# Two images in flight on one core: another order of the stages and another merge of the two streams, and routing's token sum made with the norm's transposes

## The chip, the cores and the metric

The kernel runs on one core of a Trainium2 chip. A core has a matrix engine (TensorE, PE in the profile; its weight loads are PEld), a vector engine (VectorE, DVE), a scalar engine (ScalarE, ACT), GpSimd (POOL) and SyncE (SP), which here issues all transfers. Each engine runs its own instructions in order and waits on semaphores for the others. The metric is the time of one execution on the device, in microseconds; the median of a few runs counts.

## The reference, cut to what matters

64 images of 3 x 224 x 224 go through a small vision transformer of two layers, width 192, all in float32:

```python
h = tokens(x, W, b) with class token, + pos_embed            # (64, 197, 192)
h = h + attn0(layernorm(h))      # one head: softmax(q k / sqrt(192)) v
h = h + moe(layernorm(h))        # top 1 of 3 experts for each IMAGE, gelu, width 768
h = h + attn1(layernorm(h))      # 12 heads of 16, projection with bias
h = h + ffn1(layernorm(h))       # patches: gelu MLP of width 768; 6 first tokens: routed atoms

# in moe: the image's mean over its tokens chooses the expert
scores = softmax(mean(x, axis=1) @ Wg.T);  sel = top_1(scores)
out    = (gelu(x @ W1[sel] + b1[sel]) @ W2[sel] + b2[sel]) * scores[sel]
```

The mean over tokens is what the change calls the token sum: the kernel sums the 197 tokens and divides by 197 afterwards.

## The kernel before, in words

An image's 197 tokens lie as two tiles of 99 rows (one of padding). Two images are in flight, one for each of two streams, "a" (p = 0) and "b" (p = 1); each stream has its own buffers and its own four PSUM banks. 32 pairs of images go through. What is done for an image is a list of 57 named stages, STAGES. The names that matter here:

- x: the pixels of both images are transposed by PE in six parts, DVE and ACT copy them to xT in turn (L991, L1207). tok0, tok1: the token matmuls; DVE adds the position (L994).
- statN, normN, turnN: layer norm N. stat is DVE's bn_stats and bn_aggr (L967, L972), then a power on POOL (L600, L602); norm is four tensor_scalar on DVE (L981); turn is PE's transposes (L680), a copy of the high part by ACT (L1216) and the low part by DVE (L1007). Norms 1 and 4 are turned into tokT, norms 2 and 3 into xnT.
- q0, v0, s0, p0, o0: attention 0. q0's result is copied by ACT (L1210) and its remainder made by DVE (L1013).
- route: the expert's choice. DVE sums xnT's transposes over the tokens (xsum, L1037), PE multiplies by Wg, and seven small DVE instructions with one ACT exponential give the expert and its weight (L1040 to L1054). load: SP loads that expert's weights, 2.1 MB, the first part into the tile `shared`.
- hid0_0 to hid0_2, out0_0, out0_1: the expert. hid1, out1: the MLP of layer 1.
- qk1_0, qk1_1, v1: q, k and v of attention 1. ACT copies a high part (hi, L1240), DVE makes a low part (low, L1066), and SP stacks both by nine transfers into q_stack and the k part of `shared` (L516 to L522).
- max0 to max5, maxT: row maxima of the scores of two heads each (PE L809, DVE L1075); maxT turns them and SP places them (L525, L526).
- att0 to att13: scores of head s (PE L827) and its exponential on ACT (L1251); att5, att9 and att13 also multiply the values of four heads (PE L840) and DVE normalizes them: shuffle, reciprocal, multiply (L1084, L1086, L1088). This is called a head group below.
- proj: projection (PE), added to the residual by DVE (L1091).
- regroup: seven copies on POOL that prepare the next pair's pixels.

The streams are half a pair apart: stream b begins at stage B_FIRST = 30. A string MERGE says, letter by letter, whether the next stage is taken from a's list, from b's or from the regroups. The merged list ORDER is one for all engines: each runs its part of every stage in that order, in a loop over the pairs. No engine can take a later stage first, and PE's next stage starts when its semaphores allow, so the order alone decides what stands between a producer and its consumer. A stage's name in AHEAD means that it belongs to the next image of the stream.

In the order before, the middle of a period reads, with b's stages primed and the regroups left out:

```
... att12' turn2' att13' qk1_0 qk1_1 v1 stat1 route' norm1 proj' load' turn1 stat4' q0 v0
norm4' max0 turn4' max1 max2 hid1_0' hid1_1' max3 hid1_2' max4 max5 out1_0' out1_1' ...
```

and the same with the streams changed half a period later. "First half" below is the half with a's qk1_0 and max0, "second half" the one with b's.

What waits for what, on PE: route for xsum, proj for the third head group's normalization, turn1 for norm1, q0 for tokT, max0 for the stacking transfers, for v0's copy and for q0's remainder. load's transfers wait for proj, since they overwrite the k part of `shared`.

## Time and profile before

| | |
|---|---|
| median of 3 runs | 3438.12 us (3432.95 to 3445.44) |
| the profiled execution, its own time | 3436.12 us |
| its span, first to last instruction | 3434.3 us |
| busy share | PE 85%, PEld 77%, DVE 59%, ACT 39%, POOL 10% |
| mean granted clock of PE | 0.932 of full |
| transfers | 287.5 MB, mean 84 GB/s |

Busy time is the time in which an engine's instructions run. Matmuls are pipelined and a waiting matmul can count as busy, so PE's idle time is read from the timeline as well: a number in square brackets there is the idle time of the engine before the instruction, with what ended it. "xN" is a count of instructions merged into the row. PEclk is the share of full clock that PE was granted in the stretch: 1.0 is 2.4 GHz, 0.5 is 1.2 GHz. In a windows row the columns are the stretch, its length, then busy time and instruction count of each engine in the order of the header, PEclk, the mean busy share of the 16 DMA engines and GB/s.

### The profile page before, as it was taken

The page shows a single profiled execution, that of the slowest core. Times are in us where ns is not written, and L with a number is a line of the kernel's source. Part 1 is how long each engine was busy: PE and PEld are TensorE (multiplying, and loading weights), DVE is VectorE, ACT ScalarE, POOL GpSimd, SP SyncE. Part 2 cuts the span into 40 slices and gives each one's busy share as a digit, 9 for nine tenths or more (in the row PEclk, how much of TensorE's full clock was granted, in tenths as well). Part 3 has the DMA queues.
Part 4 walks back from the last instruction along what each step waited for, and adds up shares of the span by engine and source line. Part 5 has one row for each costly group of instructions (what it writes and reads, how often), then busy time and mean ns, then how long its engine had stood idle before and what let it go on. Part 6 is the DMA issues. An engine that isn't in the chain of part 4 may idle for free.

```text
span 3434.3 us, 64029 instructions
## 1 busy us (share of the span) xinstructions
PE 2907.5 (85%) x23190; PEld 2647.5 (77%) x23190; DVE 2032.5 (59%) x5286; ACT 1347.6 (39%) x2840; POOL 356.6 (10%) x746
## 2 busy tenths in 40 slices
PE   4688888888888898888888988888898888888748
PEld 3588878877887787778878887788788778877646
DVE  4365566566656655666566656665655666566424
ACT  2144434444443344344434444443344444433311
POOL 0111111101111110111111101111111011110000
PEclk9699999999999999999999999999999999999868
DMA  5333443344243424433433344334433443333330
GB/s 148 81 66 90 91 89 71 85 98 96 64 92 83 93 65 96 96 74 82 98 82 77 81 96 96 72 84 93 87 68 88 98 96 67 89 84 83 59 87 4
DMA packets 127222, 287.54 MB, mean 84 GB/s; under 512 B 28790, under 2 KB 95367, under 8 KB 116172
## 3 DMA queue, kind: packets, MB, share of 16 engines
q1 hardware_dynamic: 127180, 286.97, 37.2%
q8 instruction: 27, 0.44, 0.1%
q14 instruction: 15, 0.12, 0.0%
HBM read 192.23 MB, written 15.00 MB: 60 GB/s over the span
## 4 chain that ended last, share of the span: by engine, by line
PE 46%; DVE 30%; DMA 9%; issue 6%; SPq 5%; ACT 3%; DVEq 0%; POOL 0%; POOLq 0%; ACTq 0%
PE banks L656 24%; PE banks L704 11%; DVE inv L1086 7%; DVE hx L981 5%; PE banks L809 4%; DMA shared<-low 4%; DMA shared<-nmaxT 4%; DVE nmax L1075 3%; DVE stats L967 2%; PE banks L827 2%; DVE sums L1084 2%; DVE xnT L1007 2%; SPq L525 2%; PE banks L680 1%; DVE low L1066 1%
## 5 line engine op out<-in xcount | busy, mean ns | idle before, releaser
L1075 DVE TENSOR_REDUCE nmax<-banks 99x4 f32<-99x788 f32 x384 | 360.7, 975 | 127.8 <-PE banks L809 122.5
L1251 ACT ACTIVATE probs_rest<-banks 99x396 f32<-99x396 f32 x512 | 246.0, 501 | 321.3 <-PE banks L827 320.0
L600 POOL TENSOR_TENSOR var_eps<-moments,eps 99x2 f32<-99x2 f32 x256 | 49.7, 194 | 2911.7 <-DVE moments L972 2911.7
L809 PE MATMUL banks<-shared,q_stack 128*99 128x198 f32 x1536 | 233.2, 290 | 91.2 <-DMA shared<-low 32.2
L827 PE MATMUL banks<-q_stack,shared 128*99 128x198 f32 x1536 | 285.6, 283 | 23.2 <-DMA shared<-nmaxT 19.1
L656 PE MATMUL banks<-tokT,fc_wT 128*128 128x198 f32 x1920 | 281.2, 302 | 5.1 <-DVE tokT L1007 5.0
L809 PEld LDWEIGHTS banks<-shared,q_stack 128*99 128x99 f32 x1536 | 188.1, 188 | 121.7 <-issue 63.9
L656 PE MATMUL banks<-tok_wT,xT 128*99 128x192 f32 x1536 | 273.3, 329 | 1.9 <-ACT xT L1207 1.9
L656 PEld LDWEIGHTS banks<-tokT,fc_wT 128*128 128x128 f32 x1920 | 260.8, 216 | 14.3 <-DVE tokT L1007 14.1
L1086 DVE RECIPROCAL inv<-sums 128x198 f32<-128x198 f32 x192 | 267.2, 1392 | 6.6
L704 PE MATMUL banks<-w_sb,hidT 128*99 128x192 f32 x1536 | 268.1, 326 | 0.0
L704 PE MATMUL banks<-fc_wT,hidT 128*99 128x192 f32 x1536 | 268.0, 326 | 0.0
L827 PEld LDWEIGHTS banks<-q_stack,shared 128*99 128x99 f32 x1536 | 194.5, 165 | 88.0 <-ACT probs_rest L1251 38.4
L656 PEld LDWEIGHTS banks<-tok_wT,xT 128*99 128x99 f32 x1536 | 243.8, 167 | 2.9 <-DVE xT L991 2.3
L704 PEld LDWEIGHTS banks<-w_sb,hidT 128*99 128x99 f32 x1536 | 241.1, 166 | 0.0
L704 PEld LDWEIGHTS banks<-fc_wT,hidT 128*99 128x99 f32 x1536 | 240.8, 166 | 0.0
L656 PE MATMUL banks<-xnT,shared 128*128 128x198 f32 x1536 | 229.0, 280 | 0.0
L1234 ACT ACTIVATE hidT<-banks,fc_bc 128x198 f32<-128x198 f32 x384 | 142.3, 422 | 216.7 <-PE banks L656 216.7
L1234 ACT ACTIVATE hidT<-banks,b_sb 128x198 f32<-128x198 f32 x384 | 142.3, 422 | 215.3 <-PE banks L656 214.1
L656 PEld LDWEIGHTS banks<-xnT,shared 128*128 128x128 f32 x1536 | 205.7, 195 | 0.0
L656 PE MATMUL banks<-proj_wT,headT 128*99 128x192 f32 x768 | 200.8, 417 | 2.9 <-DVE headT L1088 2.9
L1216 ACT ACTIVATE tokT<-banks 128x396 fp32r<-128x396 f32 x128 | 64.0, 500 | 353.8 <-PE banks L680 353.8
(189 smaller groups left out, 5435.4 us busy)
## 6 DMA issues: line engine op xcount, KB each, us to landing
shared<-w_split SPq DMA_DIRECT2D x64, 1188.0 KB
xin<-in_x_dram SPq DMA_DIRECT2D x32, 1176.0 KB
w_sb<-in_L_ffn_W_dram SPq DMA_DIRECT2D x64, 576.0 KB, 6.1
w_last<-w_split SPq DMA_DIRECT2D x64, 384.0 KB
q_stack<-hi SPq DMA_DIRECT2D x128, 148.5 KB
q_stack<-low SPq DMA_DIRECT2D x128, 148.5 KB
shared<-hi SPq DMA_DIRECT2D x128, 148.5 KB
shared<-low SPq DMA_DIRECT2D x128, 148.5 KB
```

What stands on the lines that cost most here:

```text
L525: sp.dma_start(q_stack[p][SLOT:SLOT + 1].bitcast(F32), nmaxT[p][0:HEADS].bitcast(F32)).then_inc(nmax_placed[p], 16)
L656: last = t_.matmul(dst, a, b, start=(j == 0), stop=(j == len(pairs) - 1))
L704: t_.matmul(b[0:R, t * D:(t + 1) * D], hidT[p][:, c, t * R:(t + 1) * R], w[:, c, :], start=(c == 0), stop=False)
L809: last = t_.matmul(b[n % 4][0:R, t * SP_:(t + 1) * SP_], q_stack[p][:, n, t * R:(t + 1) * R], k_stack[p][:, n, :], start=True, stop=True)
L827: last = t_.matmul(b[s % 2][0:R, kt * SP_:(kt + 1) * SP_], k_stack[p][:, s, kt * R:(kt + 1) * R], q_stack[p][:, s, :], start=True, stop=True)
L967: last = v.bn_stats(stats[p][:, t, :], norm_source(p, n)[:, t, :])
L981: last = v.tensor_scalar(xn[p][:, t, at:at + D - lo], norm_source(p, n)[:, t, lo:D], moments[p][:, t, 0:1], rstd[p][:, t:t + 1], ALU.subtr ...
L1007: last = v.scalar_tensor_tensor(out=dst[:, 1, k, :], in0=dst[:, 0, k, :].bitcast(F32), scalar=f, in1=b[TURN_BANK[n]][:, k * SP_:(k + 1) * ...
L1075: v.tensor_reduce(nmax1[p][:, :, 2 * j:2 * j + 2].rearrange("p t h -> p h t"), src, AX, ALU.max, negate=True).then_inc(nmax1_ready[p], 1)
L1086: v.reciprocal(inv1[p][:], sums1[p][:]).then_inc(inv1_ready[p], 1)
L1234: last = s_.activation(hidT[p][:, c, :], b[HIDDEN_BANK[layer][j]][:, (c % 2) * SP_:(c % 2 + 1) * SP_], ACT.Gelu, bias=bias[:, c:c + 1], sc ...
L1251: s_.activation(ring(p, s).rearrange("p k s -> p (k s)"), b[s % 2][0:R, 0:T * SP_], ACT.Exp).then_inc(p1_ready[p], 1)
```

## The change

STAGES is written out as one list (FLOW), and MERGE is another string. Against the list before:

- turn3 comes before tok0 and tok1; stat1 directly after tok1, and norm1 and turn1 lie between qk1_0, qk1_1, v1 and v0, instead of behind them;
- v0 comes before q0, where q0 came before v0; v0 and v1 get a wait of their own for the turned tokens;
- s0 comes before att0, p0 after att0, o0 after att2, stat2 after att3, norm2 after att6, turn2 after att10, where they were after att0, att2, att4, att4, att7 and att12; route stays after att13;
- the token sum xsum is made by DVE in stage turn2, right behind the two low parts, instead of at the start of DVE's part of route.

The work is the same: no instruction is added or taken away, but for PE's two waits. The middle of a period now reads:

```
... att8' att9' att10' turn2' tok1 stat1 att11' qk1_0 att12' att13' norm1 qk1_1 v1 route' proj'
stat4' load' turn1 v0 norm4' q0 turn4' max0 max1 hid1_0' hid1_1' max2 max3 hid1_2' out1_0' out1_1'
max4 hid0_0' max5 hid0_1' hid0_2' maxT s0 out0_0' out0_1' att0 p0 stat3' att1 att2 o0 ...
```

and half a period later, from proj on:

```
... turn2 tok1' att11 stat1' att12 qk1_0' att13 norm1' qk1_1' route v1' proj turn1' v0' stat4 q0' load norm4 max0' max1'
turn4 max2' max3' hid1_0 max4' hid1_1 max5' hid1_2 maxT' s0' out1_0 out1_1 att0' p0' att1' att2'
hid0_0 hid0_1 o0' hid0_2 att3' out0_0 stat2' out0_1 stat3 x att4' norm3 att5' att6' norm2' att7' turn3 tok0 ...
```

The diff:

```diff
--- before.py
+++ after.py
@@ -55,31 +55,16 @@
 
 
 
-def norm_stages(n):
-    return [f"stat{n}", f"norm{n}", f"turn{n}"]
-
-
-def ffn_stages(n):
-    return [f"hid{n}_0", f"hid{n}_1", f"hid{n}_2", f"out{n}_0", f"out{n}_1"]
-
-
-
-
-
-AHEAD = (["x", "tok0", "tok1"] + norm_stages(1) + ["q0", "v0", "s0", "p0", "o0"] + norm_stages(2)
-         + ["route", "load"])
-BESIDE = {0: ["s0"], 2: ["p0"], 4: ["o0", "stat2"], 7: ["norm2"], 12: ["turn2"], 13: ["route"]}
-ATTENTION = []
-for s in range(HEADS + 2):
-    ATTENTION += [("att", s)] + BESIDE.get(s, [])
-STAGES = (ffn_stages(0) + ["stat3", "x", "norm3", "tok0", "tok1", "turn3", "qk1_0", "qk1_1", "v1"]
-          + norm_stages(1) + ["q0", "v0"] + [("max", j) for j in range(HEADS // 2)] + ["maxT"] + ATTENTION
-          + ["proj", "load"] + norm_stages(4) + ffn_stages(1))
+AHEAD = ["x", "tok0", "tok1", "stat1", "norm1", "turn1", "q0", "v0", "s0", "p0", "o0", "stat2", "norm2", "turn2", "route", "load"]
+FLOW = ("""hid0_0 hid0_1 hid0_2 out0_0 out0_1 stat3 x norm3 turn3 tok0 tok1 stat1 qk1_0 norm1 qk1_1 v1 turn1 v0 q0 max0
+        max1 max2 max3 max4 max5 maxT s0 att0 p0 att1 att2 o0 att3 stat2 att4 att5 att6 norm2 att7 att8 att9 att10
+        turn2 att11 att12 att13 route proj stat4 load norm4 turn4 hid1_0 hid1_1 hid1_2 out1_0 out1_1""")
+STAGES = [(n[:3], int(n[3:])) if n[:3] in ("att", "max") and n != "maxT" else n for n in FLOW.split()]
 
 
 B_FIRST = 30
-MERGE = ("abaaaaabbbabbbbbarabbbababbbaaaababbabaababraabbabaabbbbabbaaabaarbabaabaaaabaab"
-         "barraaaabarbbbabaabababrbbabbabbabaabbbab")
+MERGE = ("baabababaaabrabbbbaabbbbaababbaaabbbbraarbrabaabbaabbbababbaabbaababaabaaaaabrrr"
+         "aabaaaababababbababbabaabbabbabababbaabbb")
 
 
 def merged_order():
@@ -741,6 +726,7 @@
                             tokens(p, None, tokT), columns(qk_fold, slice(m * 128, (m + 1) * 128)))))
                     last.then_inc(g_done[p], 1)
                 elif name == "v0":
+                    pe.wait_ge(xnT_ready[p], norm_count(1, it))
                     if not isinstance(it, int) or it:
                         pe.wait_ge(low_ready[p], 2 * it - 1)
                     values(p, it, b[1], attn_wv, tokT)
@@ -791,6 +777,7 @@
                             tokens(p), columns(qk_wT, slice(e * KC, (e + 1) * KC)))))
                     last.then_inc(qk_done[p], 1)
                 elif name == "v1":
+                    pe.wait_ge(xnT_ready[p], norm_count(3, it))
                     values(p, it, b[3], v_wT, xnT)
                 elif name[0] == "max":
                     j = name[1]
@@ -1008,6 +995,9 @@
                             out=dst[:, 1, k, :], in0=dst[:, 0, k, :].bitcast(F32), scalar=f,
                             in1=b[TURN_BANK[n]][:, k * SP_:(k + 1) * SP_], op0=ALU.mult, op1=ALU.add)
                     last.then_inc(xnT_ready[p], 1)
+                    if n == 2:
+                        v.tensor_reduce(xsum[p][:], b[TURN_BANK[2]][:, 0:2 * SP_].rearrange("p (k s) -> p k s", k=2)
+                                        [:, :, 0:SEQ], AX, ALU.add).then_inc(xsum_ready[p], 1)
                 elif name == "q0":
                     dve.wait_ge(g_high[p], it + 1)
                     v.scalar_tensor_tensor(
@@ -1033,9 +1023,6 @@
                     last.then_inc(h_ready[p], 1)
                 elif name == "route":
 
-                    dve.wait_ge(xnT_ready[p], norm_count(2, it))
-                    v.tensor_reduce(xsum[p][:], b[TURN_BANK[2]][:, 0:2 * SP_].rearrange("p (k s) -> p k s", k=2)
-                                    [:, :, 0:SEQ], AX, ALU.add).then_inc(xsum_ready[p], 1)
                     dve.wait_ge(logit_done[p], it + 1)
                     v.tensor_scalar(logit[p][:], b[3][0:R, ROUTED:ROUTED + EXPERTS], 1.0 / SEQ, None, ALU.mult).then_inc(logit_ready[p], 1)
                     dve.wait_ge(logit_ready[p], it + 1)
```

## Rows read from the trace of the kernel before

**Rows 1.** The page, part 1: busy time, share and instructions of each engine.
```profile
PE 2907.5 (85%) x23190; PEld 2647.5 (77%) x23190; DVE 2032.5 (59%) x5286; ACT 1347.6 (39%) x2840; POOL 356.6 (10%) x746
```

**Rows 2.** The DVE's token sum (L1037): count, durations, first and last start.
```profile
L1037 DVE TENSOR_REDUCE xsum<-banks x64: 532/534/569, 100.2 to 3209.4; 128x2 f32<-128x394 f32 x64
```

**Rows 3.** Windows: 1500 us in mid-run, then four stretches of one pair.
```profile
core 0: us, PE busy (x) PEld busy (x) DVE busy (x) ACT busy (x) POOL busy (x), PEclk, DMA share, GB/s
...
1000.00:2500.00 1500.00, 1316.08 (x10776) 1208.05 (x10775) 926.81 (x2433) 629.98 (x1331) 165.78 (x347) 0.95 0.38 86
...
1533.20:1546.52 13.32, 9.02 (x65) 8.13 (x63) 9.18 (x30) 3.36 (x8) 2.88 (x6) 0.87 0.87 126
1546.52:1578.89 32.37, 31.59 (x262) 29.26 (x262) 18.86 (x45) 14.88 (x33) 3.44 (x7) 1.00 0.15 59
1578.89:1593.73 14.84, 9.75 (x79) 8.51 (x79) 10.84 (x37) 3.37 (x8) 2.33 (x5) 0.89 0.83 146
1593.73:1630.60 36.87, 34.93 (x307) 31.95 (x308) 22.33 (x53) 19.56 (x38) 2.33 (x5) 1.00 0.24 72
```

**Rows 4.** Timeline of PE, qk1_0 to max0 of the first half (start, us).
```profile
1531.11 0.88 PE L840 MATMUL banks<-probs_rest,vals 99*32 99x198 f32 x16
1532.15 2.10 PE L656 MATMUL banks<-xnT,qk_wT 128*96 128x198 f32 x20 [0.16 <-DVE xnT L1007]
1534.09 1.06 PE L656 MATMUL banks<-v_wT,xnT 128*99 128x192 f32 x10
1537.17 0.60 PE L656 MATMUL banks<-wgT,xsum 128*99 128x3 f32 x4 [2.02 <-DVE xsum L1037]
...
1539.02 2.13 PE L656 MATMUL banks<-proj_wT,headT 128*99 128x192 f32 x6
...
1541.10 0.86 PE L680 MATMUL banks<-ident,hx 99*128 99x99 f32 x4
1543.36 1.36 PE L656 MATMUL banks<-tokT,qk_fold 128*128 128x198 f32 x10 [1.39 <-DVE tokT L1007]
...
1546.52 0.61 PE L809 MATMUL banks<-shared,q_stack 128*99 128x198 f32 x4 [0.90 <-DMA shared<-low]
```

**Rows 5.** Timeline of DVE, the same stretch.
```profile
1532.63 0.38 DVE L1084 STREAM_SHUFFLE sums<-banks 128x198 f32<-128x198 f32 x1
...
1534.75 1.03 DVE L1066 SCALAR_TENSOR_TENSOR low<-hi,banks 96x396 fp32r<-96x396 f32 x2
1535.70 0.61 DVE L967 BATCH_NORM_STATS2 stats<-h_tok 99x6 f32<-99x192 f32 x2
...
1536.58 0.54 DVE L1037 TENSOR_REDUCE xsum<-banks 128x2 f32<-128x394 f32 x1
1537.80 0.16 DVE L1040 TENSOR_SCALAR logit<-banks 99x3 f32<-99x3 f32 x1 [0.69 <-PE banks L656]
...
1538.98 1.11 DVE L981 TENSOR_SCALAR hx<-h_tok,moments,rstd 99x192 f32<-99x192 f32 x4
1541.34 0.56 DVE L1091 TENSOR_TENSOR hx<-banks,hx 99x384 f32<-99x384 f32 x1 [1.25 <-PE banks L656]
1542.54 0.36 DVE L1007 SCALAR_TENSOR_TENSOR tokT<-tokT,banks 128x198 fp32r<-128x198 f32 x1 [0.63 <-ACT tokT L1216]
```

**Rows 6.** Timeline of SP: first and last of nine stacking transfers.
```profile
1533.88 0.67 SPq L516 DMA_DIRECT2D q_stack<-hi  x1
...
1539.35 0.60 SPq L522 DMA_DIRECT2D shared<-low  x1
```

**Rows 7.** Timeline of PE: x's second half; max1, max2; max4, max5; att0.
```profile
1521.88 1.23 PE L721 MATMUL banks<-ident,xg 84*128 84x84 f32 x14 [0.60 <-DVE xT L991]
...
1547.52 1.31 PE L809 MATMUL banks<-shared,q_stack 128*99 128x198 f32 x8
...
1552.86 0.91 PE L809 MATMUL banks<-shared,q_stack 128*99 128x198 f32 x8
...
1563.70 0.42 PE L827 MATMUL banks<-q_stack,shared 128*99 128x198 f32 x2 [0.29 <-DMA shared<-nmaxT]
```


## The prediction

> **What bounds the kernel now.** I began with the page [rows 1]. TensorE (PE) is busy 85% of the span, more than any other engine, so the question is where the other 15% lies and whether the new order reaches it. All engines follow one written order of stages; PE stands still where a stage's input isn't made yet. The 64 token sums run from 100.2 to 3209.4 us [rows 2], 63 steps of 49.35 us: a pair of images takes 98.7 us, and 3109 us of the span are 31.5 such pairs. What a pair saves is multiplied by 31.5.
>
> Next I cut one pair (97.4 us) at two of its stages, qk1_0 and max0, into four stretches, two for each image [rows 3]. The two short ones, from the end of qk1_0 to the start of max0 (13.3 and 14.8 us), hold only 9.0 and 9.75 us of PE work; the long ones are 98% and 95% busy. The short ones are also where the granted clock is 0.87 and 0.89, that is, partly at 1.2 instead of 2.4 GHz; in the long ones it is 1.00. Over 1500 us it is 0.95 [rows 3].
>
> The timeline of PE shows the first short stretch [rows 4]: 2.02 us of waiting for the token sum, then proj, whose second half takes 2.08 us at the low clock (1539.02 to 1541.10), then 1.39 us for tokT, then 0.90 us until max0. DVE, in the same stretch [rows 5], explains the first: the token sum stands behind the third head group (1532.63 to 1534.75, 2.12), two low halves (0.95) and a statistics stage (0.88), although its input was there before them. But the last wait, the one that lets max0 go, is another: DMA, shared<-low. SP issues the nine stacking transfers from 1533.88 to 1539.35 [rows 6], and max0 starts at 1546.52, 12.6 us after the first issue. The DMA engines are 87% and 83% busy in the short stretches and 15% and 24% in the long ones [rows 3]. So taking away the 2.02 us alone would gain nothing in the first half: max0 would only wait longer for its transfers. That is what the sum has to respect.
>
> **The change, part by part.**
>
> *The token sum* costs DVE 0.54 us wherever it stands [rows 2]. Now it follows turn2 at once, with att11, qk1_0, att13, qk1_1 and v1 (some 4 us of PE work) ahead of route. PE's 2.02 us at route goes. DVE's later steps gain nothing by it: the run of work is as long.
>
> *The short stretches.* Between qk1_0's end and max0, DVE has in the new list, for the first half: stat1 0.88, low 0.48, heads 2.12, norm1 1.1, low 0.48, routing 1.18 (1537.80 to 1538.98), residual 0.56, stat4 0.88, turn1 0.65: 8.3 us [rows 5]. Then v0 and q0 on PE (2.26, from 1543.36 to max0 less its wait [rows 4]), q0's copy on ACT (0.5, an estimate: a low half on DVE takes 0.48 over as many columns [rows 5]) and its remainder on DVE (0.56, the residual's row): 11.6, with handovers some 12.3. The transfers need 0.55 for the copy that precedes them and 12.6 [rows 6, 4], together 13.1. So transfers end last, in both halves (in the second, DVE does without stat4 and is earlier). The old stretches were 13.3 and 14.8 [rows 3]; the new are 13.1 each: -0.2 and -1.75. SP is the same queue in the same order (q, k, then load), so the nine issues keep their 5.5 us.
>
> Inside them the first half now holds two pieces that stood outside: the third head group (0.88, row 1531.11 [rows 4]), which came before qk1_0 and now comes after, and turn4 (0.3 to 0.4, half of turn1's 0.86 at the low clock), now ahead of max0. They are covered by the transfers, so the long stretches lose 1.2 us of work.
>
> *q0 behind v0.* Before, v0's 1.06 us hid q0's copy and remainder; now max0 follows them, 1.1 us after q0. That is in the 12.3, so the transfers hide it by 0.8. Without that cover it would cost 1.1 in each half.
>
> *stat4 ahead of turn1* (first half) puts 0.88 of DVE work in front of tokT, for which v0 waits: also in the 12.3. *load* waits for proj and expert as before, and the same stages lie between it and hid0_0 (p0 apart), where no row shows a wait for it.
>
> *The long stretches.* Gains, first one: hid1_0 and hid1_1 now stand between max1 and max2, so that DVE's maxima (0.98 each) are done; before, max1 and max2 took 1.31 us where max4 and max5 took 0.91 [rows 7]; with what PE loses around max0 I count 0.8. s0 and both halves of out0 (5 us) now lie between maxT and att0, which had waited 0.45, of which the trace shows 0.29 [rows 7]. Losses: turn2 needs norm2, which on DVE now follows a head group (2.12) and turn3; I reckon 0.7 there and 0.2 at the next head group. With o0's shorter wait (-0.3, an estimate: DVE reaches its copy sooner) and turn4 gone (-0.35) the first long stretch comes to -1.0. In the second, the head group moved out gives -0.9 and att0's wait -0.5; against that x follows out0_1 directly, so DVE's residual (0.56) and stat3 (0.88) stand before the first copy of xT: its wait of 0.60 [rows 7] becomes some 1.35 (+0.75). max2 and max3 of the second half still wait for norm4, max0 and max1 on DVE (+0.35 over now), and the exponentials of att4 to att7 follow ACT's copies of xT (+0.3). Together 0.0. Bounds for both: -3.7, if beyond this all the idle time went that PE shows in them (0.8 and 1.9 us [rows 3]); +1.6, if none of the waits got shorter and the losses were a quarter larger (2.3 times 1.25, less 1.25 of moved work).
>
> *The sum*: -0.2 - 1.75 - 1.0 - 0.0 = -2.95 a pair, and I add -0.3 for the small waits, between 0 and the bound: -3.25. Times 31.5 that is -102 us. The profiled execution took 3436.1 (span 3434.3), 2 us under the median shown; 3436 - 102 = 3334.
>
> **A rule against it.** The clock is low only in the short stretches, with waits of 1.4 and 2.0 us, and full in the long ones, whose waits are below 0.8 [rows 3, 4, 7]. The Trainium skill (TensorE: Matmul & The Clock Gate, section "A second HAM failure mode: psum-queue depth-cycling") says that frequent micro-idles between groups of matmuls make the clock swing between its levels, at a cost paid between bursts. By that rule many small waits are no better than few large ones, and the time would be the fourth rival's. The trace doesn't bear it out for the long stretches.
>
> **The rivals.**
>
> First, a larger gain. A pair takes 98.7 on average, but the one with both falls of the clock inside the short stretches took 97.4: 1.3 us a pair are lost when a fall reaches a long stretch. In the new order the short ones wait for transfers, so a fall there is free. If the falls stay there and the small waits go to their bound: -0.2 - 1.75 - 3.7 - 1.3 = -6.95 a pair, 3217. For it: in the first half PE has 1.2 us more work in a short stretch. Against: idle time there remains a third.
>
> Second, nothing. The transfers hold the first short stretch as it is, the long ones give back 1.6, and the second keeps only -1.75: -0.35 a pair, 3425 to 3436. For it: DMA's name on max0's wait.
>
> Third, the sum isn't out of the way. It stands ahead of tok1's addition and stat1 on DVE, and everything behind it is 0.54 later; if the DVE run outgrows 13.1, proj or v0 waits as route did. That makes the short stretches 13.6 each: -2.2 a pair, 3367; inside my forecast's range.
>
> Fourth, slower: the clock. If it falls early in the run, v0 and q0 take 4.5 instead of 2.26, 12.3 becomes 14.6, and the low level reaches into the long stretches, as 0.95 on average says it sometimes does. At half clock, each us of low time in a long stretch costs half a us. It decides the sign when 6.5 us more a pair are spent low there (now 10% of 98.7, about 10, short ones included); at 10 more, +5.0 - 3.25 = +1.75 a pair, 3491. For it: v0's wait in the first half grows to some 2.2 us (residual, stat4 and turn1 after proj). Against: the idle time of the short stretches falls as a whole.
>
> **How the numbers follow.** Forecast with the third rival (3270 to 3415): 0.56. Larger gain: 0.19. Nothing: 0.10. Slower: 0.15. A measurement tells 0.3%, some 10 us. Nothing splits into 0.01 faster and 0.09 same. So faster 0.76, same 0.09, slower 0.15. The range reaches from the larger gain's end, 3215, to 3435; left out are the slower case and a little below, under 2 in 10.
>
> **What would show it.** After: no wait of route for xsum; qk1_0's end to max0 about 13.1 us in both halves, ended by DMA or by q0's remainder, with DMA above 0.85; 95.5 us a pair; a wait of some 2 us at v0, in the first half, and x's 0.60 grown to about 1.3. Wrong if max0 goes earlier than 13 us (the transfers are not the floor), if the clock is below 1.00 in long stretches, or if turn2, att9 or x wait more than 2 us together beyond what I put down.

## The result and the profile after

The changed kernel takes 3345.2 us (median of 4 runs, 3343.41 to 3349.07), the kernel before beside it on the same chip 3441.8 us (4 runs): a ratio of 0.9722, 95% interval 0.9708 to 0.9736. Forecast were 3334 us, range 3215 to 3435. The profiled execution after took 3345.71 us (span 3343.9, mean granted clock 0.937), that of before 3436.12 (0.932). In one experiment (x first, with q0 first) two of five executions ran at a lower clock, 0.934 to 0.936 in place of 0.956 to 0.962, and took some 90 us longer; its ratio leaves them out, and its profile is of one of them, so it stands in no table below.

First the page's part 1 and the token sum's row after.

```profile
PE 2851.5 (85%) x23190; PEld 2632.7 (79%) x23190; DVE 2035.6 (61%) x5286; ACT 1344.4 (40%) x2840; POOL 358.9 (11%) x746
```

```profile
L999 DVE TENSOR_REDUCE xsum<-banks x64: 558/561/564, 103.0 to 3117.7; 128x2 f32<-128x394 f32 x64
```

The instruction counts are those of [rows 1]. The sums run from 103.0 to 3117.7 us, 63 steps: 95.7 us a pair of images, against 98.7 by [rows 2]. That is 3.0 us a pair, and over 31.5 pairs 94.5 us.

The waits of PE, summed over the span (us in total, times, longest): route's for the token sum before, then those after:

```profile
PE banks L656 <- DVE xsum L1037: 134.6, 64, 2.2
```

```profile
PE banks L641 <- DVE tokT L994: 107.3, 65, 2.0
PE banks L796 <- DMA shared<-low: 103.5, 33, 3.9
PE banks L706 <- DVE xT L978: 48.1, 31, 1.6
...
PE banks L796 <- DVE xnT L1003: 23.9, 29, 0.9
...
PE banks L641 <- DVE xsum L999: 3.6, 2, 1.8
```

Route's wait for xsum, 64 times some 2 us before, is left twice. What remains is v0's wait for tokT, x's for xT, and max0's, which in the second half is for the stacking transfers (103.5 us, 33 times) and in the first for q0's remainder (23.9 us, 29 times).

One pair in four stretches, cut as in [rows 3] (end of qk1_0 to start of max0, and the rest), here beginning with the second half; and 1500 us in mid-run:

```profile
1540.85:1554.06 13.21, 8.37 (x79) 7.44 (x79) 9.53 (x34) 3.25 (x8) 1.77 (x4) 1.00 0.88 127
1554.06:1591.25 37.19, 35.06 (x291) 32.82 (x291) 21.69 (x49) 19.58 (x38) 2.37 (x5) 0.95 0.27 84
1591.25:1604.95 13.70, 10.14 (x84) 9.28 (x83) 10.60 (x35) 4.01 (x10) 3.47 (x7) 0.88 0.87 136
1604.95:1636.40 31.45, 30.73 (x262) 28.93 (x266) 19.46 (x46) 14.24 (x32) 3.44 (x7) 1.00 0.15 55
1000.00:2500.00 1500.00, 1327.31 (x11152) 1236.42 (x11150) 964.74 (x2537) 644.50 (x1365) 175.89 (x366) 0.96 0.40 87
```

The short stretches are 13.2 and 13.7 us, DMA is busy 88% and 87% in them; the long one of the second half is no longer at full clock (0.95).

The same pair on the timeline of PE, only rows with a wait:

```profile
1544.62 1.22 PE L641 MATMUL banks<-proj_wT,headT 128*99 128x192 f32 x6 [0.36 <-DVE headT L1075]
...
1548.65 1.13 PE L641 MATMUL banks<-attn_wv,tokT 128*99 128x192 f32 x10 [1.31 <-DVE tokT L994]
...
1554.06 0.96 PE L796 MATMUL banks<-shared,q_stack 128*99 128x198 f32 x8 [3.16 <-DMA shared<-low]
...
1580.72 1.23 PE L706 MATMUL banks<-ident,xg 84*128 84x84 f32 x14 [1.56 <-DVE xT L978]
...
1595.17 1.22 PE L641 MATMUL banks<-proj_wT,headT 128*99 128x192 f32 x6 [0.69 <-DVE headT L1075]
...
1599.93 1.68 PE L641 MATMUL banks<-attn_wv,tokT 128*99 128x192 f32 x10 [2.05 <-DVE tokT L994]
...
1604.95 1.00 PE L796 MATMUL banks<-shared,q_stack 128*99 128x198 f32 x8 [0.81 <-DVE xnT L1003]
```

And SP's first and last stacking issue of the second half and its first issue of load, with q0's remainder there on DVE's timeline:

```profile
1541.48 0.67 SPq L501 DMA_DIRECT2D q_stack<-hi  x1
...
1546.88 0.60 SPq L507 DMA_DIRECT2D shared<-low  x1
...
1549.08 0.40 SPq L484 DMA_DIRECT2D shared<-w_split  x1
...
1551.47 0.57 DVE L1003 SCALAR_TENSOR_TENSOR xnT<-xnT,banks 128x396 fp32r<-128x396 f32 x1 [1.99 <-ACT xnT L1197]
```

From the first issue (1541.48) to max0 (1554.06) it is 12.58 us, as in [rows 6] and [rows 4], where it was 12.6. In the second half PE is now done 3.16 us before max0 can go, and DVE's remainder (to 1552.04) 2.0 us before.

For the experiments the same cut was made through all pairs between 400 and 3000 us of each trace, from the start of qk1_0 (so that a short stretch is some 1 us longer than in the windows) to the start of max0, and on to the next qk1_0. "1" is the half with a's qk1_0, "2" the other. In brackets stands how much of a stretch PE spent at the lower clock, 1.2 GHz. Each number is a mean over 25 to 28 stretches, worked out from PE's rows and from the granted clock.

| kernel | short 1 | long 1 | short 2 | long 2 | pair (low clock) |
|---|---|---|---|---|---|
| before | 14.61 (3.73) | 32.28 (3.10) | 15.82 (2.44) | 35.94 (0.84) | 98.64 (10.10) |
| after | 14.74 (3.41) | 30.36 (0.00) | 14.26 (0.55) | 36.23 (4.17) | 95.58 (8.14) |
| sum alone | 14.40 (4.53) | 32.85 (5.32) | 14.64 (1.19) | 37.10 (4.55) | 98.98 (15.58) |
| order alone | 17.57 (5.83) | 30.47 (0.17) | 18.26 (6.42) | 36.63 (3.69) | 102.93 (16.11) |
| other merge | 14.33 (0.57) | 32.00 (3.50) | 15.69 (1.66) | 36.96 (7.22) | 98.97 (12.94) |
| after, 7 transfers | 13.90 (2.06) | 31.12 (1.60) | 12.35 (0.00) | 35.97 (2.15) | 93.34 (5.81) |
| sum alone, 7 transfers | 13.16 (2.73) | 31.65 (1.57) | 14.65 (1.56) | 36.28 (1.72) | 95.74 (7.58) |
| before, filled | 14.42 (0.00) | 32.36 (3.69) | 14.93 (0.00) | 38.64 (1.64) | 100.34 (5.32) |
| sum alone, filled | 14.40 (0.05) | 31.59 (1.72) | 14.33 (0.00) | 35.80 (0.00) | 96.12 (1.77) |
| after, filled | 14.32 (0.00) | 30.34 (0.00) | 14.26 (0.00) | 36.22 (3.15) | 95.15 (3.15) |
| 7 transfers, filled | 13.08 (0.00) | 30.54 (0.00) | 12.36 (0.00) | 36.19 (2.65) | 92.17 (2.65) |
| the same, q0 first | 13.99 (0.00) | 31.10 (0.79) | 11.86 (0.00) | 40.11 (7.88) | 97.06 (8.66) |
| after, filled, x first | 14.32 (0.00) | 30.34 (0.00) | 14.26 (0.00) | 38.07 (4.46) | 96.99 (4.46) |

A second number is of use: the mean over only those stretches in which the clock never fell. By it orders can be compared without the clock, with the caution that a mean may rest on few stretches (3 to 28; 3 in the first of before, 6 in its third). Where a kernel has none, that of its filled version stands (marked *); the two can differ by 0.2, as in the first long stretch of before (31.20, filled 30.97).

| at full clock | short 1 | long 1 | short 2 | long 2 | pair |
|---|---|---|---|---|---|
| before | 14.40 | 31.20 | 14.92 | 35.79 | 96.31 |
| sum alone | 14.40* | 30.96* | 14.32 | 35.80 | 95.48 |
| after | 14.32* | 30.36 | 14.26 | 35.00* | 93.94 |
| sum alone, 7 transfers | 12.19 | 31.24 | 14.07 | 35.78 | 93.28 |
| after, 7 transfers | 13.15 | 30.40 | 12.35 | 35.18 | 91.08 |

### The profile page after: what moved, and what is told of

Same layout as the page of the kernel before. It is cut to its first block, busy times and chain, and to the rows that moved or that the text cites. A ratio compares the mean times of both kernels' runs of the same rounds, so it can differ in the third digit from the quotient of the medians.

```text
span 3343.9 us, 64120 instructions
## 1 busy us (share of the span) xinstructions
PE 2851.5 (85%) x23190; PEld 2632.7 (79%) x23190; DVE 2035.6 (61%) x5286; ACT 1344.4 (40%) x2840; POOL 358.9 (11%) x746
## 4 chain that ended last, share of the span: by engine, by line
PE 58%; DVE 20%; DMA 8%; SPq 6%; issue 5%; ACT 3%; DVEq 0%; POOL 0%; ACTq 0%; POOLq 0%
PE banks L641 29%; PE banks L689 15%; DMA shared<-low 7%; PE banks L796 6%; DVE inv L1073 4%; DVE hx L968 3%; PE banks L814 3%; DVE stats L954 2%; PE banks L665 1%; SPq L501 1%; SPq L502 1%; SPq L506 1%; DVE sums L1071 1%; DVE xnT L994 1%; PE banks L827 1%
## 5 line engine op out<-in xcount | busy, mean ns | idle before, releaser
L796 PE MATMUL banks<-shared,q_stack 128*99 128x198 f32 x1536 | 231.8, 293 | 143.8 <-DMA shared<-low 103.5
L814 PE MATMUL banks<-q_stack,shared 128*99 128x198 f32 x1536 | 294.1, 288 | 21.6 <-ACT probs_rest L1238 13.1
L641 PE MATMUL banks<-tokT,fc_wT 128*128 128x198 f32 x1920 | 272.3, 297 | 1.3 <-DVE tokT L994 1.3
L1238 ACT ACTIVATE probs_first<-banks 99x396 f32<-99x396 f32 x256 | 124.5, 500 | 188.1 <-PE banks L814 182.7
L1046 DVE SCALAR_TENSOR_TENSOR hx<-banks,weight,h_tok 99x384 f32<-99x384 f32 x64 | 39.5, 618 | 236.7 <-PE banks L691 236.7
```

What stands on the lines that cost most here:

```text
L641: last = t_.matmul(dst, a, b, start=(j == 0), stop=(j == len(pairs) - 1))
L796: last = t_.matmul(b[n % 4][0:R, t * SP_:(t + 1) * SP_], q_stack[p][:, n, t * R:(t + 1) * R], k_stack[p][:, n, :], start=True, stop=True)
L814: last = t_.matmul(b[s % 2][0:R, kt * SP_:(kt + 1) * SP_], k_stack[p][:, s, kt * R:(kt + 1) * R], q_stack[p][:, s, :], start=True, stop=True)
L1046: v.scalar_tensor_tensor(out=h[p], in0=b[3][0:R, 0:T * D], scalar=weight[p][:, 0:1], in1=h_tok[p][:].rearrange("p t d -> p (t d)"), op0=AL ...
L1238: s_.activation(ring(p, s).rearrange("p k s -> p (k s)"), b[s % 2][0:R, 0:T * SP_], ACT.Exp).then_inc(p1_ready[p], 1)
```

## The experiments

Times are medians; the ratio is to the kernel before, run on the same chip (3443.8 to 3449.6 us). A difference in us between two experiments can hold some 8 us of the chips; where it does, the difference of the ratios stands beside it, times 3445 us.

### The two parts of the change, each alone

The sum alone: the kernel before, with the reduction moved.

```diff
                     last.then_inc(xnT_ready[p], 1)
+                    if n == 2:
+                        v.tensor_reduce(xsum[p][:], ...
...
                 elif name == "route":
-                    dve.wait_ge(xnT_ready[p], norm_count(2, it))
-                    v.tensor_reduce(xsum[p][:], ...
```

> The old order with the token sum moved into turn2, nothing else. Transfers theory (between qk1_0 and max0 the nine stacking transfers take 12.5 us from the first issue, so what is saved before them is only waited for longer): the wait of route goes, the first half's stretch stays at 13.1 to 13.3 us, the second goes from 14.8 to 13.1 at best; about 1.9 us a pair, 60 us, so 3370 to 3395 against 3441. Sum theory (the whole gain of the change is route's wait of twice 2.1 us and the low clock behind it): 3 to 4 us a pair, 3320 to 3350, as fast as the change. Order theory (the sum is worth nothing): 3441.

Measured: 3446.2 us, ratio 0.9997 (0.9985 to 1.0010): nothing, and not the 3370 to 3395 that I had put on the transfers' case. PE's waits between qk1_0 and max0, on its timeline, in the first half and in the second:

```profile
1541.73 0.56 PE L680 MATMUL banks<-ident,hx 99*128 99x99 f32 x4 [1.68 <-DVE hx L981]
...
1543.68 2.45 PE L656 MATMUL banks<-tokT,qk_fold 128*128 128x198 f32 x10 [1.39 <-DVE tokT L1007]
...
1548.78 0.98 PE L809 MATMUL banks<-shared,q_stack 128*99 128x198 f32 x4 [0.98 <-DMA shared<-low]
...
1586.94 1.22 PE L656 MATMUL banks<-proj_wT,headT 128*99 128x192 f32 x6 [0.45 <-DVE headT L1088]
...
1590.49 0.56 PE L680 MATMUL banks<-ident,hx 99*128 99x99 f32 x4 [1.18 <-DVE hx L981]
...
1595.63 0.96 PE L809 MATMUL banks<-shared,q_stack 128*99 128x198 f32 x8 [1.01 <-DMA shared<-low]
```

In the first half the 2.02 us of route [rows 4] are now 1.68 us at turn1; in the second they are 0.45 at proj and 1.18 at turn1. max0 waits for the transfers in both (in all of the first halves, in 17 of 25 second ones). At full clock the first short stretch is the same (14.40), the second 0.6 us shorter; 5.5 us more of low clock a pair take that back.

The order alone: the changed kernel, with the reduction put back into route.

```diff
-                    if n == 2:
-                        v.tensor_reduce(xsum[p][:], ...
...
                 elif name == "route":
+                    dve.wait_ge(xnT_ready[p], norm_count(2, it))
+                    v.tensor_reduce(xsum[p][:], ...
```

> The new order with the token sum put back at the start of DVE's part of route. In the new order DVE reaches route some 2.6 us after PE does (1596.53 against 1593.96 in the changed kernel), so PE waits there for about 3 us, and proj, turn1 and v0 are later by about 2 us in each half. Transfers theory: the stretches grow past the transfers, from 13.7 and 13.2 to about 15.5 and 15; +3.5 us a pair, about 3450, no better than the kernel before: the order needs the sum moved. Order theory: the order keeps most of its gain, under 3380. Sum theory: the order is worth nothing, so 3441 to 3450 as well; e1 tells these two apart.

Measured: 3548.4 us, ratio 1.0292 (1.0266 to 1.0318), where I expected about 3450. The first row is of the waits of PE, the others of the timelines of PE and DVE, from the start of qk1_0:

```profile
PE banks L641 <- DVE xsum L1024: 186.3, 64, 3.4
```

```profile
1579.56 1.10 PE L641 MATMUL banks<-xnT,qk_wT 128*96 128x198 f32 x10
...
1586.01 0.76 PE L641 MATMUL banks<-wgT,xsum 128*99 128x3 f32 x4 [2.55 <-DVE xsum L1024]
...
1585.40 0.56 DVE L1024 TENSOR_REDUCE xsum<-banks 128x2 f32<-128x394 f32 x1
```

The new order alone loses 100 us. Behind qk1_0 it puts a low half, a head group (2.12), norm1 (1.11) and another low half on DVE [rows 5] ahead of route's part. So the sum, still there, ends 6.4 us after the start of qk1_0, where it was 5.0 [rows 4, 5], and proj and all behind it are later with it. The short stretches grow to 17.6 and 18.3 us; the long ones are as in the change (30.5, 36.6). So neither part gains time alone; together they gain 97 us.

### Two of nine transfers taken out

Eight of the nine stacking transfers are large. Here the two that fill the fourth slot are left out, and with them the product of the low parts of q and k; seven remain. First from the changed kernel:

```diff
-                    sp.dma_start(dst[3 * HD:SLOT], rest).then_inc(stacked[p], 16)
...
-                        pe.wait_ge(stacked[p], 144 * it + 144)
+                        pe.wait_ge(stacked[p], 112 * it + 112)
...
-                v.memset(q_stack[p][SLOT:].bitcast(F32), 0.0)
+                v.memset(q_stack[p][:].bitcast(F32), 0.0)
```

> The changed kernel with two of the eight large stacking transfers left out, those that give q and k a second copy of their low parts (fourth slot); q's slot is zero throughout, so the product of low part with low part, the smallest of four, is left out of the scores of attention 1. Transfers theory: first issue to landing goes from 12.5 to about 10 us; max0 of the second half then waits for q0's remainder, about 1.3 us earlier; the first half, which already waits for q0's remainder, stays. 1.2 to 1.6 us a pair, 40 to 50 us, about 3300. If DVE's or PE's run holds both stretches: 3345, unchanged. If the number of issues on SP (0.6 us each) held it: 1.2 us a pair as well, but the landing would follow the last issue by the same 7 us as before.

Measured: 3261.6 us, ratio 0.946 (0.9439 to 0.9482), 84 us below the change (90 by the ratios), where I expected some 45. max0 of the second half and of the first, on the timeline of PE:

```profile
1513.17 0.96 PE L795 MATMUL banks<-shared,q_stack 128*99 128x198 f32 x8 [1.28 <-DVE xnT L1002]
...
1563.42 1.66 PE L795 MATMUL banks<-shared,q_stack 128*99 128x198 f32 x8 [0.53 <-DVE xnT L1002]
```

DMA no longer ends the wait in either half: q0's remainder does. At full clock the short stretches lose 1.2 and 1.9 us, so the transfers were the floor of both there. As the change runs, at the low clock, the first half already waited for q0's remainder.

Then the same edit on the sum alone, in the old order:

> The old order with the token sum made in turn2 (3446 us), and two of the nine stacking transfers left out in each image, with the product of the low parts that they feed. If the transfers are what ate the sum's gain, as the prediction says of the first half, max0's wait for them goes (0.98 us in the first half, 1.01 in the second, read in the trace of the sum alone) and max0 follows v0 or q0's remainder: 0.9 us less in each short stretch at full clock (13.5 and 13.4 in place of 14.4 and 14.3), 1.8 us a pair or 57 us, about 3390, and more if the clock's low time falls with the idle time. If DVE's run of work holds the stretch and DMA is only the last by name, both stay at 14.3 to 14.4 and the time within 10 us of 3446.

Measured: 3348.5 us, ratio 0.9737 (0.9702 to 0.9771), 98 us below the sum alone (90 by the ratios). At full clock the first short stretch goes from 14.40 to 12.19, over twice what I expected, the second only from 14.32 to 14.07. So in the first half the transfers had held back the gain of the sum. How much of the 2.2 us is the sum's isn't shown, since the kernel before wasn't run with seven transfers; its max0 waited for the transfers 0.90 us in the first half [rows 4] and 1.1 in the mean of those that did (24 of 26), so an estimate is that at least 1.1 us is the sum's. In the second half the old order is held by DVE's run of work, as PE's waits there show:

```profile
1544.88 0.56 PE L679 MATMUL banks<-ident,hx 99*128 99x99 f32 x4 [1.18 <-DVE hx L980]
...
1546.76 1.37 PE L655 MATMUL banks<-tokT,qk_fold 128*128 128x198 f32 x10 [1.32 <-DVE tokT L1006]
...
1549.81 0.98 PE L808 MATMUL banks<-shared,q_stack 128*99 128x198 f32 x8 [0.78 <-ACT vals L1219]
```

Turn1 and q0 wait for DVE, max0 for v0's copy on ACT, none for DMA. It is the new order that shortens this half (to 12.35, once the transfers allow it).

### Unread matmuls in PE's waits

To see what the clock is worth, matmuls that nobody reads (198 columns of a weight tile, into a bank that the next stage overwrites) fill the waits. They add work for PE and take nothing away. After, 16 and 10 of them ahead of v0's wait in the two halves, 6 and 24 ahead of max0's:

```diff
+            def fill(b, n):
+                for _ in range(n):
+                    t_.matmul(b[0:R, 0:SP_], fc1_wT[:, 0, 0, 0:R], fc1_wT[:, 0, 0, 0:SP_], start=True, stop=True)
...
+                    fill(b[1], (16, 10)[p])
                     pe.wait_ge(xnT_ready[p], norm_count(1, it))
...
+                        fill(b[0], (6, 24)[p])
                         pe.wait_ge(stacked[p], 144 * it + 144)
```

> The changed kernel with matmuls whose results nobody reads put where PE waits: 16 and 10 of 198 columns ahead of v0's wait in the first and second half, 6 and 24 ahead of max0's; some 0.11 us each. No other work is touched. Clock theory (idle time of PE in the short stretches brings the clock to its low level, and where that reaches a long stretch each us there costs half a us): the low time, 8.1 us a pair, of which 4.2 lie in the second long stretch, goes to near 0; the second long stretch gets 2 us shorter, the first short one 0.3 to 0.6; 2 to 2.6 us a pair, 65 to 80 us, 3265 to 3285. Transfers alone (the clock doesn't matter, since the low time is where PE waits anyway): 3345, or up to 30 us more where the filling overshoots.

Measured: 3327.7 us, ratio 0.9648 (0.9631 to 0.9664), 17 us below the change (25 by the ratios), clock 0.962 in place of 0.937. Low clock falls from 8.1 to 3.2 us a pair, the pair only from 95.58 to 95.15 us: 0.4 us for 5.0 us less of low clock, far less than the 65 to 80 us in all that I had put on the clock. The second long stretch is as long as it was (36.22). max0 of the second half and of the first, on the timeline of PE:

```profile
1547.18 0.96 PE L802 MATMUL banks<-shared,q_stack 128*99 128x198 f32 x8 [0.97 <-issue]
...
1597.63 0.98 PE L802 MATMUL banks<-shared,q_stack 128*99 128x198 f32 x8 [1.03 <-DMA shared<-low]
```

"issue" stands for a wait in which the profile shows nothing that PE waited for.

The sum alone, with 13 and 9 ahead of turn1's wait, 10 ahead of q0's, 7 ahead of max0's:

> The old order with the token sum in turn2 (e1), with unread matmuls ahead of turn1's wait (13 and 9), q0's (10) and max0's (7). If the clock took what the sum saved (e1: short stretches 1.4 us a pair shorter, low time in the long ones up from 3.9 to 9.9 us), then with the clock held the long stretches lose up to 5 us: 3290 to 3320. If the old order itself lengthened the long stretches: no faster than 3420.

Measured: 3360.7 us, ratio 0.9744 (0.9728 to 0.9761), clock 0.969 in place of 0.907. Low clock falls from 15.6 to 1.8 us a pair, and the time by 86 us, with 24982 matmuls in place of 23190. I expected 3290 to 3320.

The kernel before, with 16 ahead of route's wait, 10 ahead of q0's, 6 ahead of max0's:

> The kernel before with unread matmuls ahead of route's wait (16), q0's (10) and max0's (6), the sum where it was. Clock theory: the long stretches lose half of their 3.9 us of low time, 2 us a pair; the short ones stay, since route's wait does: 3370 to 3395. Against e7 it gives what the sum is worth at a held clock: by the transfers theory 1.4 to 1.9 us a pair, 45 to 60 us; by the sum theory 4 us, 125 us.

Measured: 3490.1 us, ratio 1.013 (1.0083 to 1.0176), clock 0.952. Low clock falls from 10.1 to 5.3 us, but the pair is longer, by a wait at the loop's start that the trace of before doesn't have there (timeline of PE, hid0_0):

```profile
1531.53 0.69 PE L656 MATMUL banks<-xnT,shared 128*128 128x198 f32 x4 [1.96 <-issue]
```

So this run doesn't tell what the old order is worth at a steady clock. Its second short stretch at full clock (14.93) does agree with that of before (14.92).

Seven transfers with 16 and 10 unread matmuls ahead of v0's wait, 4 and 9 ahead of max0's, the product of low parts left out:

> e5 (six large stacking transfers instead of eight; the product of the two low parts is left out of the scores of attention 1) with unread matmuls ahead of v0's wait (16 and 10) and max0's (4 and 9). Clock theory: 5.8 us of low time a pair, 3.8 in the long stretches, go: 1.9 us, 60 us, about 3200. Without the clock: 3262.

Measured: 3227.5 us, ratio 0.9357 (0.9341 to 0.9372), the fastest of all, where I expected about 3200. Of those that compute all of it, the change with unread matmuls is the fastest (3327.7).

### Steps of the order

Another merge: after max0 of the first half the letters are changed so that stat4, load and norm4 of the other stream stand ahead of q0, and turn4 and hid1_0 ahead of max0, in the second half. The same letters take hid1_2 ahead of max4, so that nothing stands between max5 and maxT any more.

```diff
-         "aabaaaababababbababbabaabbabbabababbaabbb")
+         "aabaaaababababbababbaaabaabbabbabbbbaabbb")
```

> The changed kernel with the end of MERGE changed: stat4, load, norm4 ahead of the other stream's q0, and turn4 and hid1_0 ahead of its max0, so that 1.5 us of PE work stands in the 3.16 us in which max0 of the second half waits for its transfers. Transfers theory: max0 of the second half starts where it did, or up to 0.5 us later, 13.2 to 13.7 us after qk1_0, the work behind it is 1.5 us shorter, and the maxima follow each other more closely; 1.0 to 1.6 us a pair, 30 to 50 us, 3295 to 3315. If instead DVE's run of work holds that stretch, norm4 ahead of q0's remainder makes max0 later by norm4's 1.1 us or more and nothing is gained: 3340 to 3360.

Measured: 3438.2 us (10 executions, 3405 to 3444), ratio 0.9953 (0.9929 to 0.9978). My expectation failed by over 120 us. PE's waits in the second half, on its timeline:

```profile
1589.95 1.13 PE L641 MATMUL banks<-attn_wv,tokT 128*99 128x192 f32 x10 [1.31 <-DVE tokT L994]
...
1593.11 0.56 PE L665 MATMUL banks<-ident,hx 99*128 99x99 f32 x4 [0.92 <-DVE hx L968]
...
1594.99 1.36 PE L641 MATMUL banks<-tokT,fc_wT 128*128 128x198 f32 x10 [1.32 <-DVE tokT L994]
...
1602.74 0.39 PE L802 MATMUL banks<-ident,nmax 99*128 99x99 f32 x2 [1.59 <-DVE nmax L1062]
```

In place of 3.16 us at max0 there are 0.92 at turn4, 1.32 at hid1_0 and a new wait of 1.59 at maxT, for DVE's maxima, where hid1_2 had stood between. So the gap moved rather than went: the waits of PE of 0.15 us and more, added up over the stretches, are 11.9 us a pair where the change has 10.8. At full clock the second short stretch is 0.8 us longer (15.05, 10 stretches, against 14.26), as I had put it for the case that DVE's run holds it. The rest goes with the clock: low clock rose from 8.1 to 12.9 us a pair, and both long stretches grew (the second short one is 15.69 in the mean). Its own executions go with the clock: 3443.5 us at a mean of 0.915, 3418.6 at 0.925, 3405.1 at 0.929.

q0 ahead of v0 again, on the fastest kernel (4 unread matmuls ahead of max0 in both halves):

```diff
-        ... qk1_1 v1 turn1 v0 q0 max0
+        ... qk1_1 v1 turn1 q0 v0 max0
```

> The kernel with six transfers and unread matmuls (3227.5 us), with q0 ahead of v0 again; the product of low parts is left out as there. In that kernel's trace max0 waits 0.45 us in both halves, for q0's remainder, while its six transfers have landed. If q0's copy and remainder hold max0 there, v0's 1.06 us now hides them: 0.5 to 0.9 us a pair less, about 3200 to 3215 us. If the transfers hold it (they take 9.7 us from the first issue), nothing changes: 3224 to 3230 us, and max0's wait is put down to DMA.

Measured: 3377.4 us, ratio 0.9801 (0.9785 to 0.9817): 150 us slower, where I expected 12 to 27 faster. The second short stretch is 0.5 us shorter, as expected; the first is 0.9 us longer (13.08 to 13.99). And DVE's timeline shows, in the second half:

```profile
1562.69 0.57 DVE L1010 SCALAR_TENSOR_TENSOR xnT<-xnT,banks 128x396 fp32r<-128x396 f32 x1 [1.99 <-ACT xnT L1204]
1563.17 0.61 DVE L961 BATCH_NORM_STATS2 stats<-hx 99x6 f32<-99x192 f32 x2
1563.89 0.25 DVE L966 BATCH_NORM_AGGREGATE moments<-stats 99x2 f32<-99x6 f32 x2
1565.30 1.11 DVE L975 TENSOR_SCALAR hx<-hx,moments,rstd 99x192 f32<-99x192 f32 x4 [1.17 <-POOL rstd L586]
```

q0's remainder waits 1.99 us for PE and ACT, and stat4 and norm4 of the other stream are queued behind it. PE then stands at turn4, in the first half inside the short stretch and in the second outside:

```profile
1518.83 0.56 PE L664 MATMUL banks<-ident,hx 99*128 99x99 f32 x4 [1.33 <-DVE hx L975]
...
1566.48 0.56 PE L664 MATMUL banks<-ident,hx 99*128 99x99 f32 x4 [1.73 <-DVE hx L975]
```

The second long stretch grows by 3.9 us, and low clock in it from 2.7 to 7.9 us.

The same with x ahead of stat3 (b's stat3 moves with it, behind att1):

```diff
-        ... out0_0 out0_1 stat3 x norm3 turn3 ...
+        ... out0_0 out0_1 x stat3 norm3 turn3 ...
```

> The kernel of the run before, with stage x ahead of stat3 instead of behind it, so that DVE makes its first copy of xT before it takes stat3's statistics (0.88 us). By the prediction's step on x, its wait of 1.56 us comes of stat3 and shrinks to about 0.6. If norm3, turn3 and turn2, which follow stat3 on DVE, have slack, that is 0.95 us a pair or 30 us less than the run before; if turn2 (or the next head group) then waits that much longer, 0.3 us a pair or less, under 10 us.

Measured: 3334.8 us (median of the three executions that the ratio goes by), ratio 0.9674 (0.9651 to 0.9696), 43 us less than the run before. But the clock differs too between these two (0.956 to 0.962 against 0.933 to 0.939), so this run doesn't tell what x first is worth. Its timeline shows x's wait at 0.57 us and a new one of 1.85 at turn3.

So x first was run again on the changed kernel with unread matmuls, q0 behind v0:

> The new kernel with unread matmuls (3327.7 us), with stage x ahead of stat3, q0 behind v0 as in the change. By what the run of x first with q0 first showed, x's wait shrinks from 1.56 to about 0.57 us, and turn3 then waits some 1.85 us for norm3, which stat3 makes later: +0.85 us a pair at full clock, 27 us, about 3350 to 3360. If instead x's wait is what the change loses in the second long stretch, the time falls by 0.95 us a pair, to about 3298. The clock can add or take 10 to 20 us in either case, so the waits of the timeline decide.

Measured: 3379.6 us, ratio 0.9816 (0.9791 to 0.9840), 52 us slower than without (58 by the ratios). x and turn3 on the timeline of PE:

```profile
1588.13 1.24 PE L710 MATMUL banks<-ident,xg 84*128 84x84 f32 x14 [0.56 <-DVE xT L984]
...
1593.32 0.56 PE L665 MATMUL banks<-ident,hx 99*128 99x99 f32 x4 [1.87 <-DVE hx L974]
```

The wait of 1.56 became 0.56 and 1.87. At full clock the second long stretch goes from 35.00 to 36.08 (+1.1, 34 us in all; the second number rests on 3 stretches); 1.3 us more of low clock go with the rest.

## Why the prediction was right, step by step

The forecast was 11 us below the measured time. Its mechanism held: the sum out of PE's way, the transfers as the floor of the short stretches, and a smaller gain in the long ones. Two terms were mis-sized, and they cancelled; that the total came so near is in part luck. One of the signs by which I would have been wrong did come: the clock is below 1.00 in a long stretch (0.95 in the second).

**The transfers hold the short stretches.** Shown for the second half, and for the first at full clock. Taking out two of nine shortens both in the new order (by 1.2 and 1.9 us at full clock), and in the old order with the sum moved the first by 2.2. The stretches I put at 13.1 each are 13.21 (second) and 13.70 (first) in the profiled pair; 0.63 us of the 13.21 pass before the first issue, where I put 0.55. In the first half, as the change runs, the last wait is for q0's remainder in all 27 stretches, 0.8 us, with v0 and q0 partly at the low clock: 13.1 us from the first issue to max0, where the transfers take 12.6. With the clock held it is DMA, 1.03 us. I had named both ends.

**The sum alone gains nothing in the first half.** Right, and the whole time is unchanged too (0.9997), but the reason covers only the first half. In the second, whose max0 waited for v0's copy and not for the transfers before, the sum is worth 0.6 us a pair at full clock, 19 us in all, and the low clock took these back.

**Short stretches, -0.2 and -1.75.** Measured +0.13 and -1.56 in the mean, -0.1 and -0.66 at full clock. The second term was mis-sized in its kind: I read 14.8 from one pair [rows 3], whose stretch was at a clock of 0.89, and took all of it for the order's. Of the 1.56, 0.66 is order, and the rest goes with 1.9 us less of low clock.

**Long stretches, -1.0 and 0.0.** Measured -1.92 and +0.29 in the mean, -0.84 and -0.79 at full clock. The first matches at full clock; the rest of it is 3.1 us of low clock that is gone from there. The second was mis-sized: the order gains 0.8 us there, and 3.3 us more of low clock take it back, behind the 3.16 us in which PE waits for the transfers. Of my own terms, x's wait is 1.56 where I put 1.35, turn2's 0.18 where I put 0.7.

**The sum, -3.25.** Measured -3.06 in the mean of the pairs. At full clock it is -2.37 (96.31 to 93.94), and low clock, down from 10.1 to 8.1 us a pair, makes the other 0.7. My -0.3 "for the small waits" stood, by luck, in the place of a part of it.

**q0 behind v0, costed at nothing under the transfers.** That the transfers hide it wasn't tested by itself: the swap was run only with seven of them. Without their cover I put 1.1 us in each half, and that was too much: with q0 first the second short stretch is 0.5 us shorter there, the first 0.9 us longer. The view was also too narrow, since DVE then has norm4 queued behind q0's remainder, and turn4 waits for it (1.33 us in the first half, 1.73 in the second); v0 first gives DVE its time for norm4, and in the second half for stat4.

**The clock as a rival, slower.** It didn't happen here, but the mechanism is real and I gave it too little weight. Moving the sum alone raised low clock from 10.1 to 15.6 us a pair, another merge of the same stages to 12.9. Filling the sum alone's waits, with the order unchanged, gave 86 us back. Of the 3.40 us a pair between the sum alone and the whole change, 1.54 are order (95.48 to 93.94) and the other 1.86 come with 7.4 us less of low clock. The price a us: the long stretches, regressed on their low time, give 0.2 to 0.5 us for each us at 1.2 GHz (0.6 in one kernel). The Trainium skill (TensorE: Matmul & The Clock Gate, section "HAM oscillation — how this bites in real kernels") reckons half the throttled time as the penalty. The slopes are mostly below that, 0.37 in the first long stretch of before, and the fill of the change gave under 0.1 us for each us of low clock that it took away; that a part of the slower work lies under waits is likely and not shown. By the Trainium skill's section "A second HAM failure mode: psum-queue depth-cycling" on the same page, small idle times between groups of matmuls made the clock of one kernel swing. The second half of the sum alone, in which one wait of some 2 us became two smaller ones, agrees with it (low clock 3.3 to 5.7 us); its first half, in which the wait stayed one (2.02 to 1.68 us), has more low clock as well (6.8 to 9.9), and the change, with small waits too, has less (8.1 a pair).

**What stays open.** Which of PE's idle places sets where the clock falls. How much PE stands idle in all doesn't tell it: the waits of 0.15 us and more come to 11.9 us a pair before, 11.2 in the sum alone, 10.8 after and 11.9 in the other merge, and low clock to 10.1, 15.6, 8.1 and 12.9. So where the clock takes or gives back a part of a gain is measured here, and why it does so is not. That the fills brought waits put down to "issue" is open too.

## What to carry to other kernels

Before a wait is taken away, look for what ends second: here a transfer did in one half and DVE's run in the other, and two edits that were worth 0 and -100 us alone gained 97 together. When a small part of the engines' order is swapped, read what is queued behind the moved instruction on DVE as well as on PE; both swaps tried on the faster order took away 1 us of waiting or less and brought a longer wait elsewhere. Keep two means of every stretch, over all pairs and over those at full clock: the difference goes with the clock, and a term read from one pair may hold more of it than of the change.

## What the runs showed of the hardware that I had not expected

- The same instructions in three similar orders ran at a mean granted clock of 0.907 (sum alone), 0.915 (other merge; 0.915 to 0.929 over its ten executions) and 0.937 (after).
- Matmuls that nobody reads made kernels faster: 8% more of them, 86 us less in the sum alone (clock 0.907 to 0.969), 17 us in the change (25 by the ratios; 0.937 to 0.962), and 5% more, 34 us less with seven transfers (0.944 to 0.963).
- The same kind of added matmuls brought waits put down to "issue" that hadn't been there: 1.96 us at the loop's start of the old order, 0.97 us at max0 of the new one.
- The stacking transfers took the same 12.6 us from first issue to max0 in both orders, in stretches where they ended last, with the expert's weights issued on the same queue before they had landed (in the change from 1549.08 us on, 5.0 us before max0).
